# Causal zeros by GpSimd in place of mask matmuls in an attention and experts kernel

## The reference

```python
scores = jnp.einsum('bqhd,bkhd->bhqk', qq, kk) * scale
causal = jnp.tril(jnp.ones((S, S), dtype=bool))
scores = jnp.where(causal[None, None], scores, jnp.finfo(scores.dtype).min)
probs = jax.nn.softmax(scores, axis=-1)
y = jnp.einsum('bhqk,bkhd->bqhd', probs, v).reshape(B, S, H)
```

## Time and profile before

| | |
|---|---|
| runs | 499.88, 499.88, 500.12 us (median 499.88) |
| profiled execution | span 498.5 us from first to last instruction; no separate time of it is listed |
| PE busy | 438.1 us (88%), 4044 matmul records |
| DVE busy | 364.8 us (73%) |
| ACT busy | 264.8 us (53%) |
| POOL busy | 63.9 us (13%) |
| chain that ended last | PE 52%, DVE 27%, issue 7%, DMA 5%, ACT 4% |
| mean granted TensorE clock | 0.965 |

### The profile page before, as it was taken

One profiled execution on the slowest core, in us unless ns is written; L12 is line 12 of the kernel. 1 busy time (PEld: TensorE's weight loads), 2 busy tenths in 40 slices (PEclk: granted clock), 3 DMA queues, 4 the chain that ended last, 5 costly groups with the idle time before them and its releaser, 6 DMA issues.

```text
span 498.5 us, 10894 instructions
## 1 busy us (share of the span) xinstructions
PE 438.1 (88%) x4044; PEld 232.8 (47%) x4044; DVE 364.8 (73%) x1049; ACT 264.8 (53%) x486; POOL 63.9 (13%) x56
## 2 busy tenths in 40 slices
PE   2667569899999999999999997899998999987995
PEld 2323233345445356354545544454545545654653
DVE  6566288388767887796768785667687775788886
ACT  5236247545876663778865375776543444221110
POOL 7233002433000220110002030000010000010000
PEclk9997599899999999999999998999999999999898
DMA  6037300016600124700001355000400000000000
GB/s 202 9 75 157 43 2 2 3 34 151 103 3 3 34 46 88 122 3 2 3 2 22 71 122 75 3 3 2 130 1 3 2 1 23 1 21 1 1 21 22
DMA packets 21124, 20.05 MB, mean 40 GB/s; under 512 B 2856, under 2 KB 19752, under 8 KB 20680
## 3 DMA queue, kind: packets, MB, share of 16 engines
q1 hardware_dynamic: 21072, 19.36, 18.7%
HBM read 10.70 MB, written 7.47 MB: 36 GB/s over the span
## 4 chain that ended last, share of the span: by engine, by line
PE 52%; DVE 27%; issue 7%; DMA 5%; ACT 4%; SPq 3%; POOL 1%; DVEq 0%; ACTq 0%; POOLq 0%
PE bank_A L1071 7%; PE bank_c L1034 6%; PE bank_A L1000 6%; PE bank_B L1020 5%; PE bank_M L1082 5%; DVE x L943 4%; DMA q_stack<-in_c_rows 4%; DVE k_diag L923 4%; DVE k_diag L928 3%; PE bank_B L1115 3%; PE bank_M L986 3%; PE bank_M L1089 2%; DVE differences L819 2%; SPq L468 2%; PE bank_A L1121 2%
## 5 line engine op out<-in xcount | busy, mean ns | idle before, releaser
L672 ACT ACTIVATE p_mla<-bank_B 128x512 f32<-128x512 f32 (+1 forms) x176 | 97.4, 561 | 78.9 <-PE bank_B L1023 77.1
L819 DVE CUSTOM_DVE_ANT_0 differences<-masks,bank_A 128x384 bf16<-128x384 bf16 (+1 forms) x128 | 78.4, 612 | 18.7 <-PE bank_A L1000 13.4
L651 ACT ACTIVATE pT_loc<-sT_loc 32x512 f32<-32x512 f32 x136 | 85.1, 625 | 4.5 <-DVE sT_loc L846 3.1
L1000 PE MATMUL bank_A<-k_stack,q_stack 128*128 128x128 bf16 (+3 forms) x256 | 70.1, 307 | 14.5 <-DMA q_stack<-in_c_rows 8.0
L1020 PE MATMUL bank_B<-q_stack,k_stack 128*128 128x512 bf16 (+3 forms) x256 | 67.9, 302 | 1.0 <-DVE k_diag L923 0.8
L1115 PE MATMUL bank_B<-xrT,k_diag 128*128 128x512 f32 x128 | 63.7, 612 | 3.7 <-DVE k_diag L923 3.2
L839 DVE TENSOR_REDUCE row_max<-bank_A 128x16 f32<-128x512 f32 (+1 forms) x36 | 24.8, 690 | 39.4 <-PE bank_A L1071 39.2
L1071 PE MATMUL bank_A<-k_diag,qT 128*32 128x512 f32 x272 | 49.7, 757 | 0.0
L1023 PE MATMUL bank_B<-masks 128*128 128x128 bf16 x256 | 49.1, 219 | 0.0
L1000 PEld LDWEIGHTS bank_A<-k_stack,q_stack 128*128 128x128 bf16 x256 | 25.6, 100 | 49.9 <-issue 26.4
L1034 PE MATMUL bank_c<-p_mla,v_mla 128*9 128x128 f32 (+3 forms) x512 | 47.0, 437 | 1.4 <-ACT p_mla L672 1.4
(11 more groups left out here) (137 smaller groups left out, 624.8 us busy)
## 6 DMA issues: line engine op xcount, KB each, us to landing
parts_dram<-parts SPq DMA_DIRECT2D x16, 192.0 KB, 2.7
k_stack<-parts_dram SPq DMA_DIRECT2D x8, 384.0 KB
q_stack<-parts_dram SPq DMA_DIRECT2D x8, 384.0 KB
parts_dram<-parts SPq DMA_DIRECT2D x16, 128.0 KB, 2.7
k_diag<-kT SPq DMA_DIRECT2D x64, 18.0 KB
x<-in_x SPq DMA_DIRECT2D x4, 256.0 KB, 7.6
parts_dram<-parts SPq DMA_DIRECT2D x16, 64.0 KB, 2.3
out<-x SPq DMA_DIRECT2D x4, 256.0 KB, 2.2
```

What stands on the lines that cost most here:

```text
L651: last = nc.scalar.activation(pT_loc[rows, :, rows], sT_loc[rows, t % 2, :].rearrange("p (h k) -> p h k", h=H), ACT.Exp, scale=SCALE)
L672: drained_by(nc.scalar.activation(p_mla[:, n % P_RING, m:m + len(heads), j * P:], src, ACT.Exp, scale=SCALE), step)
L819: drained_by(nc.vector.tensor_tensor_reduce(differences[:, 0:w], masked16[:, S - w:], bank[:, 0:w], -1.0, -NEG, ALU.add, ALU.min, dst), step)
L1000: last = nc.tensor.matmul(bank[:, n * w:(n + 1) * w], q_stack[b % 2][:, h // 2, h % 2, i * P:(i + 1) * P], k_stack[b % 2][:, h // 2, 0:w], ...
```

## The change

The matmul with the mask goes, and the score matmul stands alone (`stop=True`). The exp is then taken of all scores of the diagonal block, the future ones too. At the place of each values' step in the list, POOL waits for the exp of the block's last unit and runs one affine select over the diagonal blocks of the four heads (128 partitions x 4 x 128, f32, in place), which keeps q >= k and writes 0 elsewhere. The values' matmuls wait for that select in place of the exp. In the list, PV moves behind all units of the next block.

```diff
-                steps += units[:1] + late + units[1:]
+                steps += units + late
...
+        future_cut = sem("future_cut")
...
                 if step == ("MB", 1, 0):
                     clear(1)
+                if step[0] == "PV":
+                    _, b, g, j = step
+                    n = pv_no[step]
+                    wait_drained(pool, ("E", b, g, j, len(exp_units(g, j)) - 1))
+                    diagonal = p_mla[:, n % P_RING, :, j * P:(j + 1) * P]
+                    nc.gpsimd.affine_select(diagonal, diagonal, [[0, 4], [1, P]], ALU.is_ge, 0.0, base=0,
+                                            channel_multiplier=-1).then_inc(future_cut, 1)
                 if step[0] == "MB" and step[1] == 0:
...
-                        nc.tensor.matmul(bank[:, m * w:(m + 1) * w], k_stack[b % 2][:, h // 2, j * P:(j + 1) * P],
-                                         q_stack[b % 2][:, h // 2, h % 2, j * P:], start=True, stop=False,
-                                         skip_group_check=True)
-                        last = nc.tensor.matmul(bank[:, m * w:m * w + P], eye16, causalT16,
-                                                start=False, stop=True, skip_group_check=True)
+                        last = nc.tensor.matmul(bank[:, m * w:(m + 1) * w], k_stack[b % 2][:, h // 2, j * P:(j + 1) * P],
+                                                q_stack[b % 2][:, h // 2, h % 2, j * P:], start=True, stop=True,
+                                                skip_group_check=True)
...
-                    wait_drained(pe, ("E", b, g, j, len(exp_units(g, j)) - 1))
+                    pe.wait_ge(future_cut, n)
```

## The result

The changed kernel takes 538.28 us (median, 537.58 to 538.77, 4 runs); the kernel before took 499.88 us beside it. The ratio is 1.0782, 95% interval 1.0753 to 1.081: slower by 38 to 39 us. The profiled execution spans 536.3 us.

A forecast was written before the change was run, and what follows sets the result against it. It took PE and DVE handing banks to and fro as the bound, PE more often waited for. 42.4 - 2.1 - 11 + 3 - 8 - 3 = +21 us on 499.9 gave about 520 us, range 505 to 545.

The forecast's parts named there:

- eight stops behind POOL's jobs: At eight values' steps PE waits until an older POOL job and the select behind it are done; sum 36.2 us.
- small ones: Twelve more values' steps where the select alone is late, by 0.02 to 1.25 us each; 6.2 us added.
- DMA wait ahead of S(3,0) absorbs: PE's `q_stack` DMA wait hangs on a POOL split, not on PE's stop behind it, so 2.1 us are absorbed.
- given back after stops: DVE and ACT empty their queues during stops, so PE then finds banks free; 11 us back, bounds 5 and 20.
- clock: Matmuls run at half speed for a while after three long stops; 1 us each, 3 us, bounds 0 and 8.
- masks gone and later values' steps: 256 mask matmuls leave PE's queue, 8 us off; moved values' steps wait less for the exp, 3 us off.
- upper of two near rows: Select's price on POOL, taken from a same-size cast, 610 ns, and a tensor_tensor, 1159 ns; 1.16 us chosen.
- The later place: Values' steps moved later in PE's queue lose their waits for the exp; 3 us off, bounds 0 and 5.
- the 15 us of queue: Most that PE's queue could shorten without the masks: 256 matmuls at 0.06 us; the upper bound of that gain.
- Rival 3: The select is quick and more comes back after the stops; about 508 us, chance 0.22.
- Rival 4: The select is slow, 2.4 us, and nearly every values' step waits for POOL; about 548 us, chance 0.18.
- Rival 1: POOL's stops are absorbed, over 31 of 42 us, and PE's queue gets shorter; 492 us, chance 0.09.

The follow-up runs named there:

- the better POOL order: The changed kernel with each select placed on POOL where the block's last exp unit stands, ahead of splits and adds; 499.13 us, ratio 1.0008.

## Why the prediction came out as it did

The direction, the mechanism and the places were right; 538.28 us lies in the range, near its top, and not in the forecast's own 513 to 530. Here is the account that the runs give, against the sum's terms:

| term | predicted, us | shown, us |
|---|---|---|
| eight stops behind POOL's jobs | +36.2 | +31.7 |
| small ones | +6.2 | +1.8 (select in exp order over no select: 0.4 + 1.4; in the changed kernel itself PE's matmuls wait for POOL nowhere but at the eight) |
| DMA wait ahead of S(3,0) absorbs | -2.1 | -2.1 (the shorter of two waits is gone) |
| given back after stops | -11 | about 0 |
| clock | +3 | +9 |
| masks gone and later values' steps | -8 - 3 = -11 | -1.4 together (-5.0 + 3.6) |
| sum | +21 | +39.0, measured +39.0 |

The terms on the right come from several pairs of kernels, each known to 1 or 2 us, so that the sum fits to the tenth is chance; that it fits within 2 us is not.

*Price of the select.* I took the upper of two near rows, 1.16 us and so 1.3 with the handoff; it is 0.64 and 0.76, at the lower bound of 0.75. Eight stops at 0.54 us less are 36.2 - 4.3 = 31.9 us, and 31.7 were measured, so the subtraction of PE's places from POOL's job ends was right to 0.2 us in the sum. Single stops are right within 0.2 us, except that behind LN(3), which measured 0.6 us more. The estimates from the Trainium skill (GPSIMD Engine Reference, section 7), 0.87 and 0.44 us, lie on either side of the measured 0.635, nearer to it than my choice.

*What comes back.* This is the step that failed most. I argued that free banks give 1 us for each stop. The doubled select shows 7.2 us more waiting and 7 us more time, so little or nothing comes back there. In the sum, the changed kernel lies 38.6 us above the one with the better POOL order (1.0782 - 1.0008 = 7.74%); less 8.7 for the clock (1.0782 - 1.0608) that is 29.9 us. Against it stand 31.7 us of stops less the DMA wait ahead of S(3,0), which is 2.7 us in that kernel, 29.0. Nothing came back in the sum, to within 1 or 2 us. There was some of the cover that I had counted on, as PE's waits for DVE over the whole kernel are 42.1 us against 44.3 with the better order, but that is 2 us and not 11.

*The clock.* One us for each of three stops was far too little. There are 33 us more at half clock, and filling five stops won 9 us. Not three but seven stops, from 2.4 us on, had half clock behind them.

*The later place* had the wrong sign. That PE waits less for the exp was right, but not that this is all it does. The 3 us were too much even for what they stood for: values' matmuls alone had waited 1.4 us for the exp, the rest of the 5.3 being the weight loads' share. At the late place PE waits longer for DVE in the score pass, 15.5 against 9.5 us with masks and 20.9 against 17.5 without. Why it does was not isolated and stays open.

*The masks*: 8 us were on the chain; 5.0, 5.9 and 7 us came off in the three pairs of kernels, so there the chain's share was a fair guide and the 15 us of queue were not.

The errors of price and small stops (33.5 in place of 42.4, -9) and of masks and later place (+9.6) nearly cancel, which is luck; what is left, 11 + 6 us, is the give-back and the clock, and 520 + 17 + 1 is 538.

Rival 3 (a quick select) had the right price and a wrong rest: 508 us was worked out with 16 us given back. Rival 4's time, 535 to 548 us, came true with the price wrong. Rival 1 falls, since of the stops next to nothing was absorbed, and not over 31 us.

A version faster than before was not found. The kernel without masks and zeros, 494.3 us, marks what free zeros would be worth here; with selects 499.1 us was the best, the same as with the masks.

## What to carry to other kernels

Work that is moved to a nearly idle engine still joins that engine's queue. Before moving it, list the jobs that will stand ahead of it in the queue, take from the trace when each ends, and compare that with when the busy engine needs the result: that subtraction gave the eight stops, and their sum within 1% once the select's price was known. Where a job stands ahead that itself waits for the busy engine's latest output, put the new work in the order in which its input is ready, not in the order in which its output is wanted; that one edit was worth 38 us here. And count a stop of TensorE of over 2 us as more than its length, since the matmuls behind it ran at half clock for 3 to 6 us here: 32 us of stops brought 9 us on top.

## What the runs showed of the hardware

- An affine select on GpSimd, 128x512 f32 in SBUF with a four-by-128 pattern and a stride of 512 elements, takes 634 to 645 ns, next to a cast of the same size (610 ns) and half a two-input tensor_tensor (1159 ns).
- With eight stops of PE in an otherwise dense stretch, the granted clock was 0.50 around or behind the seven of 2.4 to 6.7 us and 1.00 behind the one of 0.96 us. Matmuls of a zero block in the stops kept it at 1.00, though all their products are zero.
- In the kernel with the stops the same 3788 matmuls were busy for 10.4 us longer (435.4 against 425.0 us, with 68 and 20 us at half clock; a part of it is the stops themselves, which leave less overlap), so PE's busy time by itself does not tell that work was saved.
